# Issuing four read-back transfers behind the record of tile 47 in place of that of tile 49, in a fused scan and mixture-of-experts kernel

## The chip, the cores and the metric

The kernel runs on one core of one Trainium2 chip. The metric is the device time of one execution in microseconds (us), lower is better. Before the change three runs took 391.05, 392.11 and 394.93 us, a median of 392.11 us.

A core has five engines, each with an instruction queue of its own that runs in order: TensorE (PE, with weight loads shown as PEld), VectorE (DVE), ScalarE (ACT), GpSimd (POOL) and SyncE (SP). An engine at a wait does nothing of what stands behind that wait. SP issues nearly all the plain transfers (its row of the trace is called SPq), POOL the indirect ones.

## The reference, cut to what matters

The input is x of shape (8, 512, 128). It is normalised, and the result goes two ways: through a gated state-space branch with a recurrence over 512 time steps, and through a feed-forward branch with a top-2 mixture of 8 experts.

```python
def step(state, bc):                       # the recurrence, a state of 64 numbers per batch
    b_t, c_t = bc
    s = state @ A_bar + b_t
    s = _layernorm(s, ln_st_g, ln_st_b)
    return (s, c_t * s)

topw, topi = jax.lax.top_k(logits, K)      # K = 2 of E = 8
topw = jax.nn.softmax(topw, axis=-1)
w_dense = jnp.sum(jax.nn.one_hot(topi, E, dtype=xn.dtype) * topw[..., None], axis=-2)
h = _gelu(jnp.einsum('bsd,edh->ebsh', xn, ew1) + eb1[:, None, None, :])
eo = jnp.einsum('ebsh,ehd->ebsd', h, ew2) + eb2[:, None, None, :]
moe_out = jnp.einsum('ebsd,bse->bsd', eo, w_dense)
...
gate = jax.nn.sigmoid(combined @ gc_w + gc_b)
mixed = abel_out * (1.0 - gate) + moe_out * gate
...
x = x + s * g                              # s: state-space branch, g: silu of the expert branch
```

## The kernel before

**The recurrence.** The 512 steps of each batch are cut into 16 segments (`SEG`), so 128 segments of 32 steps run side by side, one in each partition, and the pass over the 32 steps is repeated in 5 rounds so that the segments' starts settle. That makes 148 steps in a row. One step is a small matrix product on PE (`tensor_step`, L1086), then on DVE the next state (L999) and its transpose `wT` (L987), which the next product waits for. Between two rounds there is a boundary (L1091, L1092 and the DVE work behind them).

**The experts.** Every token has two experts. Token rows are sorted by expert into tiles of 128 rows, in two halves of 39 tiles (`HALF_TILES`): tiles 0 to 38 are the first four batches, 39 to 77 the last four. A tile needs one *record*, the weights of its expert (`record<-experts`, a transfer by `fetch(g)`, five places in `record`), and its sorted rows (`desk<-sorted_rows` in the rows of the trace, `load_rows(c)` for three tiles at a time, 128 x 3 x 129 numbers of four bytes, which is 193.5 KB). On PE a tile is `rows_transpose` (L1520), `layer1` (L1527, the first instruction that reads the record) and `layer2` (L1537 and L1538, which raises `rows_done`). POOL then writes the finished rows back to their tokens' places in DRAM (`rows_back`, L1748, in the order of the tiles).

**What sets the order.** PE, ACT, DVE and POOL walk through the 148 steps in program order, and fixed tables say what stands behind the small product of a step t. `SLOT_AT` places the tiles: the slot with number j runs `layer1(j - 2)`, `rows_transpose(j)` and `layer2(j - 3)`. For the place in question:

| step t | what PE does behind the product of that step |
|---|---|
| 74, 75, 76, 77, 78 | slots 45 to 49: layer1 of tiles 43 to 47, layer2 of tiles 42 to 46 |
| 79 | no slot; `C_proj(0)` (L1512) |
| 80, 81, 82, 83 | slots 50 to 53: layer1 of tiles 48 to 51 |
| then | boundary of the round |

**The mix.** Once all tiles of a half are back in DRAM, `pull(n)` reads the two expert rows of every token of batch n (L1804, 516 KB each, destination `pulls[:, n % 4]`). `pull(0)` first waits until all rows of tiles 0 to 38 have landed (L1800). DVE's `factor_part(dve, n, 0)` (L1245) is the first reader, at step `MIX_AT[n]`: 79, 86, 93 and 100 for batches 0 to 3. It stands inside step 79, ahead of that step's L999.

**SP's queue.** SP's loop over the tiles g issues `fetch(g + 5)`, which waits for `rows_done` of tile g (that is, for layer2 of tile g), at every third g also `load_rows(g // 3 + 3)`, and at one g the four pulls of the first half:

```python
for g in range(TILES):
    if g + RECORDS < TILES:
        fetch(g + RECORDS)
    if g % CHUNK == 0 and g // CHUNK + 3 < TILES // CHUNK:
        load_rows(g // CHUNK + 3)
    if g == HALF_TILES + 5:
        for n in range(NB // HALVES):
            pull(n)
```

With `HALF_TILES` = 39 the pulls come at g = 44, behind the record of tile 49. The chunk of rows issued at g = 42 is number 17, that at g = 45 is number 18 (tiles 54 to 56).

Of the kernel before, what the change touches and what calls it, by code (L numbers as in the profile page):

```python
# [40 lines left out]
def build(nc, I, out):  # L41
    NB, T, H = I["L0_attn_x"].shape
    S = I["L0_attn_A"].shape[0]
    E, _, F = I["L0_ffn_ew1"].shape
    NROT = I["L0_ffn_gens"].shape[0]
    K = F // P
# [6 lines left out]
    HALF_TILES = Q * P * 2 // ROWS + E - 1  # L53
# [9 lines left out]
    with ExitStack() as ctx:  # L63
        sems = {}

        def sem(name):
            if name not in sems:
                sems[name] = ctx.enter_context(nc.semaphore(name))
            return sems[name]
# [1099 lines left out]
        def fallback(eng, one_round, redo):  # L1169

            eng.wait_ge(sem("agreed"), 1)
            settled = eng.value_load(agreed[0:1, 0:1], min_val=0, max_val=1)
            with eng.If(settled < 1):
                if one_round is not None:
                    with eng.Fori(0, SEG) as r:
                        one_round(eng, r)
                redo(eng)
            eng.end_ifs()
# [83 lines left out]
        def value_part(dve, n, i):  # L1262
            _, _, _, a, rest_g = factors(n)
            v = values[n % 4]
            part, s = divmod(i, SUB)
            if i == 0:
                dve.wait_ge(sem("factor"), factors_before(n) + 5)
                dve.wait_ge(sem("mix_rows"), n + 1)
            elif s == 0:
                dve.wait_ge(sem("value_part"), 2 * n + part)  # L1270
            if part < 2:
                t = dve.scalar_tensor_tensor(out=v[:, s, :], in0=pulls[:, n % 4, s, part, 0:P], scalar=a[:, s, part:part + 1], in1=v[:, s, :],
                                             op0=ALU.mult, op1=ALU.add)
                if s == SUB - 1:
                    t.then_inc(sem("value_part"), 1)
            else:
                t = dve.scalar_tensor_tensor(out=v[:, s, :], in0=abel[:, n, s, :], scalar=rest_g[:, s:s + 1], in1=v[:, s, :],
                                             op0=ALU.mult, op1=ALU.add)
                if s == SUB - 1:
                    t.then_inc(sem("ffn"), 1)  # L1280
# [5 lines left out]
        def summed_part(dve, n, s):  # L1286
            _, _, _, _, twice_g = factors(n)
            v = values[n % 4]
            if s == 0:
                dve.wait_ge(sem("factor"), factors_before(n) + 4)  # L1290
                dve.wait_ge(sem("base"), n - SUMMED + 1)
                dve.wait_ge(sem("summed"), n - SUMMED + 1)
            t = dve.scalar_tensor_tensor(out=v[:, s, :], in0=summed_bank(n)[:, s * P:(s + 1) * P], scalar=twice_g[:, s:s + 1], in1=v[:, s, :],
                                         op0=ALU.mult, op1=ALU.add)
            if s == SUB - 1:
                t.then_inc(sem("ffn"), 1)
# [143 lines left out]
        def store(sp, again, n):  # L1440
            sp.wait_ge(sem("final_rows"), NB * again + n + 1)
            sp.dma_start(out.rearrange("b (q k) h -> (b q) k h", k=L)[:, n * SUB:(n + 1) * SUB, :], outb[:, n]).then_inc(sem("out_stored"), 16)
# [41 lines left out]
        with nc.Block() as block:  # L1484
# [291 lines left out]
            @block.sync  # L1776
            def _(sp):
                def fetch(g):
                    e = sp.value_load(expert_of[0:1, g:g + 1], min_val=0, max_val=E - 1)
                    if g >= RECORDS:  # L1780
                        sp.wait_ge(sem("rows_done"), g - RECORDS + 1)
                    sp.dma_start(record[:, g % RECORDS], experts[:, ds(e, 1), :].squeeze(1)).then_inc(sem(f"record{g % RECORDS}"), 16)

                def load_rows(c):
                    h, t = divmod(c * CHUNK, HALF_TILES)
                    if t == 0:
                        sp.wait_ge(sem(f"scattered{h}"), 16 * 2 * Q)
                    if c >= 3:
                        sp.wait_ge(sem("rows_seen"), (c - 2) * CHUNK)
                        sp.wait_ge(sem("token_rows"), c - 2)  # L1790
                    at = (c % 3) * CHUNK
                    sp.dma_start(rows_in[:, at:at + CHUNK, :], sorted_rows[h][t * ROWS:(t + CHUNK) * ROWS, :].rearrange("(c p) h -> p c h", p=P))\
                      .then_inc(sem(f"rows_in{c % 3}"), 16)

                def pull(n):
                    h, i = divmod(n, NB // HALVES)
                    if i == 0:
                        for p in range(OUT_PLACES):
                            done = len(range(p, (h + 1) * HALF_TILES, OUT_PLACES))
                            sp.wait_ge(sem(f"rows_out{p}"), 16 * done)  # L1800
                    if n >= 4:
                        sp.wait_ge(sem("ffn"), n - 3)
                    first = JUNK + i * 2 * T
                    sp.dma_start(pulls[:, n % 4], token_rows[h][first:first + 2 * T, :].rearrange("(p s j) w -> p s j w", p=P, j=2)).then_inc(sem(f"pulled{n % 4}"), 16)  # L1804

                front_sync(sp)
                sp.wait_ge(sem("ew1_loaded"), 16)
                sp.wait_ge(sem("ew2r_ready"), E)
                sp.wait_ge(sem("eb2_stored"), 32)
                sp.wait_ge(sem("slots_ready"), 1)  # L1810
                sp.wait_ge(sem("tiles_known"), 2)
                for g in range(RECORDS):
                    fetch(g)
                for c in range(3):
                    load_rows(c)
                for g in range(TILES):
                    if g + RECORDS < TILES:
                        fetch(g + RECORDS)
                    if g % CHUNK == 0 and g // CHUNK + 3 < TILES // CHUNK:
                        load_rows(g // CHUNK + 3)  # L1820
                    if g == HALF_TILES + 5:
                        for n in range(NB // HALVES):
                            pull(n)
                for n in range(NB // HALVES, NB):
                    pull(n)
                for n in range(NB):
                    store(sp, 0, n)
                fallback(sp, None, store_redo)
                sp.wait_ge(sem("out_stored"), 16 * NB)
# [28 lines left out]
```

## Time and profile before

| | |
|---|---|
| three runs | 391.05, 392.11, 394.93 us |
| the profiled execution | 391.37 us, of which the span of the trace 389.5 us |
| mean granted TensorE clock | 0.907 of full speed |
| PE busy | 323.7 us (83%) |
| PEld busy | 250.0 us (64%) |
| DVE busy | 285.1 us (73%) |
| ACT busy | 190.8 us (49%) |
| POOL busy | 162.1 us (42%) |
| SP's DMA queue (q1) | 42.52 MB, 37.7% of the 16 DMA engines |
| POOL's DMA queue (q0) | 9.39 MB, 7.5% |

Times inside the trace count from the start of the span. A timeline row gives the start, the length, the engine, the line of the kernel and the operation, and in brackets how long the engine had been idle before it and what ended that idle time. In the row of an SP transfer the length is that of issuing; when the data has landed is another number ("to landing", counted from the issue's start). PEclk of 1.00 is the full clock of 2.4 GHz, 0.50 is 1.2 GHz.

### The profile page before, as it was taken

What the parts mean: (1) busy time and instruction counts of PE and PEld (TensorE: products, weight loads), DVE (VectorE), ACT (ScalarE), POOL (GpSimd) and SP (SyncE); (2) the same over time, 40 slices, a digit from 0 to 9 for tenths busy, and PEclk for the clock granted to TensorE, in tenths of its full rate; (3) what the DMA queues carried; (4) which work ended last, traced back from release to release, by engine and by line L of the source; (5) the groups of instructions that cost most, each with busy time, mean ns of one, the idle gap of its engine ahead of it and who ended that gap; (6) DMA issues with size and microseconds to landing.
All of it is one profiled execution on the core that took longest, in us unless ns stands there. A gap on an engine that the chain in (4) does not pass through costs nothing.

```text
span 389.5 us, 11592 instructions
## 1 busy us (share of the span) xinstructions
PE 323.7 (83%) x4002; PEld 250.0 (64%) x4014; DVE 285.1 (73%) x1320; ACT 190.8 (49%) x563; POOL 162.1 (42%) x225
## 2 busy tenths in 40 slices
PE   1886988967988869999989999889999988878770
PEld 0676975667555547887777887667767746656450
DVE  2787546999388776888857665669899755788972
ACT  1142982500033325666637668458776628565310
POOL 8051000016777777777776554335554500000000
PEclk9998995865599988999989999889999988999996
DMA  8449990001511314767757667946665224000102
GB/s 276 96 138 199 171 143 0 2 3 34 200 56 57 112 56 162 248 228 248 240 179 234 229 223 241 329 141 210 226 204 211 70 68 164 29 29 29 40 18 87
DMA packets 44158, 54.80 MB, mean 141 GB/s; under 512 B 6841, under 2 KB 28768, under 8 KB 44096
## 3 DMA queue, kind: packets, MB, share of 16 engines
q1 hardware_dynamic: 38975, 42.52, 37.7%
q0 software_dynamic: 4544, 9.39, 7.5%
q10 hardware_dynamic: 576, 2.10, 1.5%
q8 instruction: 35, 0.57, 0.6%
q14 instruction: 28, 0.22, 0.2%
HBM read 14.15 MB, written 16.63 MB: 79 GB/s over the span
## 4 chain that ended last, share of the span: by engine, by line
PE 59%; DVE 24%; issue 5%; ACT 5%; DMA 3%; SPq 2%; DVEq 0%; ACTq 0%
PE bank L1086 11%; PE bank L1527 11%; PE bank L1537 8%; PE bank L1557 2%; PE bank L1490 2%; DVE wT L987 2%; PE bank L1520 2%; PE bank L1505 2%; PE bank L1497 2%; DMA record<-experts 2%; PE bank L459 2%; PE bank L419 2%; PE bank L1426 2%; PE bank L1512 2%; PE bank L445 1%
## 5 line engine op out<-in xcount | busy, mean ns | idle before, releaser
L1748 POOL DMA_INDIRECT token_rows<-rows_out,token_rows_i x78 | 75.7, 971 | 64.2 <-ACT rows_out L1659 27.4
L1086 PE MATMUL bank<-Mrep,wT 32*32 32x64 f32 x2368 | 65.4, 225 | 17.9 <-DVE wT L987 17.6
L1086 PEld LDWEIGHTS bank<-Mrep,wT 32*32 32x32 f32 x2368 | 41.7, 107 | 55.5 <-issue 53.3
L1734 POOL DMA_INDIRECT sorted_rows<-late,slots x64 | 62.7, 980 | 28.4 <-issue 14.5
L1652 ACT ACTIVATE desk<-bank,record 128x128 f32<-128x128 f32 x156 | 48.8, 364 | 44.5 <-PE bank L1527 44.1
L1527 PE MATMUL bank<-desk,record 128*128 128x128 f32 x312 | 58.6, 313 | 0.1
L999 DVE SCALAR_TENSOR_TENSOR ring<-bank,Rho,Dv 128x64 f32<-128x64 f32 x112 | 31.8, 284 | 26.8 <-PE bank L1086 24.4
L1537 PE MATMUL bank<-record,desk 128*128 128x129 f32 x312 | 50.3, 285 | 0.0
L1527 PEld LDWEIGHTS bank<-desk,record 128*128 128x128 f32 x312 | 43.1, 200 | 7.9 <-issue 1.2
L1537 PEld LDWEIGHTS bank<-record,desk 128*128 128x128 f32 x312 | 43.4, 201 | 0.2
L1644 ACT ACTIVATE desk<-bank,cols 128x128 f32<-128x128 f32 x78 | 35.9, 460 | 3.0 <-PE bank L1520 3.0
L987 DVE STREAM_TRANSPOSE wT<-ring 128x64 f32<-128x64 f32 x112 | 27.5, 245 | 3.5
L1520 PE MATMUL bank<-ident,desk 128*128 128x128 f32 x78 | 22.4, 287 | 1.4 <-ACT desk L1644 1.4
L1659 ACT COPY rows_out<-bank 128x129 f32<-128x129 f32 x78 | 21.3, 273 | 4.3 <-PE bank L1538 4.3
L973 DVE CUSTOM_DVE_ANT_0 sqj<-ring,guess 128x64 f32<-128x64 f32 x64 | 19.6, 306 | 0.1
L459 PE MATMUL bank<-desk 128*128 128x128 f32 x72 | 13.2, 339 | 7.0 <-DVE desk L770 4.9
L1538 PE MATMUL bank<-record,ones 128*128 128x129 bf16 x78 | 17.7, 227 | 0.0
L999 DVE SCALAR_TENSOR_TENSOR late<-bank,Rho,Dv 128x64 f32<-128x64 f32 x31 | 8.7, 281 | 11.3 <-PE bank L1086 11.3
L459 PEld LDWEIGHTS bank<-desk 128*128 128x128 f32 x72 | 11.4, 241 | 8.6 <-DVE desk L770 6.4
L1557 PE MATMUL bank<-bias,ones 128*128 128x512 bf16 x46 | 15.1, 449 | 2.1 <-issue 2.1
L419 PE MATMUL bank<-B_wT,gi 128*128 128x64 f32 x64 | 12.8, 385 | 3.6 <-DVE Dv L712 3.6
L419 PEld LDWEIGHTS bank<-B_wT,gi 128*128 128x128 f32 x64 | 12.5, 297 | 4.2 <-DVE gi L707 3.7
(333 smaller groups left out, 635.9 us busy)
## 6 DMA issues: line engine op xcount, KB each, us to landing
record<-experts SPq DMA_DIRECT2D x78, 290.5 KB
sorted_rows<-zero_rows SPq DMA_DIRECT2D x2, 2515.5 KB, 28.3
desk<-sorted_rows SPq DMA_DIRECT2D x26, 193.5 KB
pulls<-token_rows SPq DMA_DIRECT2D x8, 516.0 KB, 5.4
X<-in_L_attn_x ACTq DMA_DIRECT2D x4, 512.0 KB, 6.2
out<-xT SPq DMA_DIRECT2D x8, 256.0 KB, 2.0
token_rows<-rows_out,token_rows_i POOLq DMA_INDIRECT x78
experts<-in_L_ffn_ew SPq DMA_DIRECT2D x1, 1024.0 KB, 6.4
```

The source lines that it names most:

```text
L419: t = pe.matmul(banks[bank][:, k * S:(k + 1) * S], x, w, start=True, stop=True)
L459: t = pe.matmul(banks[1][:, m * P:(m + 1) * P], XT[:, m, :], EX[:, m, :], start=True, stop=True)
L987: dve.transpose(wT[:, :], prev).then_inc(sem("state_T"), 1)
L999: dve.scalar_tensor_tensor(out=state(r, k), in0=psY, scalar=Rho[:, k:k + 1], in1=Dv[:, k, :], op0=ALU.mult, op1=ALU.add).then_inc(sem("sta ...
L1086: t = pe.matmul(psY[q], wT[q, 32 * c:32 * c + 32], Mrep[q, c, :], start=(c == 0), stop=(c == 1))
L1520: pe.transpose(bank_in[:, 0:P], rows_in[:, g % (3 * CHUNK), 0:P], ident[:, :]).then_inc(sem("rows_seen"), 1)
L1527: t = pe.matmul(hidden_bank(g)[:, k * P:(k + 1) * P], w[:, k * P:(k + 1) * P], rows_T[:, g % 2, :], start=True, stop=True)
L1537: pe.matmul(o, hidden[:, g % 2, k, :], w[k], start=(k == 0), stop=False)
L1644: act.activation(rows_T[:, g % 2, :], bank_in[:, 0:P], ACT.Identity, scale=col["ln_gamma"], bias=col["ln_beta"]).then_inc(sem("rows_T"), 1)
L1652: t = act.activation(hidden[:, g % 2, k, :], hidden_bank(g)[:, k * P:(k + 1) * P], ACT.Gelu, bias=bias[:, k:k + 1])
L1734: pool.indirect_dma_start(sorted_rows[h], bass.IndirectOffsetOnAxis(ap=slots[:, j, q:q + 1], axis=0), sort_rows[:, q, :], None)\
L1748: pool.indirect_dma_start(token_rows[h], bass.IndirectOffsetOnAxis(ap=token_rows_i[:, g:g + 1], axis=0), rows_out[:, g % OUT_PLACES, :], N ...
```

## The change

The four pulls move from iteration g = 44 to g = 42 of SP's loop.

```diff
@@ -1818,7 +1818,7 @@
                         fetch(g + RECORDS)
                     if g % CHUNK == 0 and g // CHUNK + 3 < TILES // CHUNK:
                         load_rows(g // CHUNK + 3)
-                    if g == HALF_TILES + 5:
+                    if g == HALF_TILES + 3:
                         for n in range(NB // HALVES):
                             pull(n)
                 for n in range(NB // HALVES, NB):
```

The instructions of PE, DVE, ACT and POOL stay the same and in the same order. On SP, around iterations 42 to 45, two records change places with the pulls. The row that opens this piece of the difference is the load of rows chunk 17; the rows with a minus are the records of tiles 48 and 49 (a register load of the expert's number, and the transfer), where they stood before:

```order
 L1792 DMA desk<-sorted_rows 128x3x129
-L1779 TENSOR_LOAD expert_of
-L1779 ISA x2
-L1782 ISA
-L1782 DMA record<-experts 128x581
-L1779 TENSOR_LOAD expert_of
-L1779 ISA x2
-L1782 ISA
-L1782 DMA record<-experts 128x581
 L1804 DMA pulls<-token_rows 128x1032 x4
```

In the changed kernel nothing stands between chunk 17 and the pulls, and the same two records, marked with a plus, come behind them, ahead of the record of tile 50, which opens with the last two rows:

```order
 L1804 DMA pulls<-token_rows 128x1032 x4
+L1779 TENSOR_LOAD expert_of
+L1779 ISA x2
+L1782 ISA
+L1782 DMA record<-experts 128x581
+L1779 TENSOR_LOAD expert_of
+L1779 ISA x2
+L1782 ISA
+L1782 DMA record<-experts 128x581
 L1779 TENSOR_LOAD expert_of
 L1779 ISA x2
```

So each pull is issued two records earlier in SP's order, and the records of tiles 48 and 49 four pulls later.

## Rows read from the trace of the kernel before

**Rows 1.** The page, chain that ended last: share of the span by engine.
```profile
PE 59%; DVE 24%; issue 5%; ACT 5%; DMA 3%; SPq 2%; DVEq 0%; ACTq 0%
```

**Rows 2.** Timeline of DVE at step 79.
```profile
241.29 0.16 DVE L951 SCALAR_TENSOR_TENSOR Rho<-roots,Rho 128x1 f32<-128x1 f32 x1
243.93 0.17 DVE L1245 TENSOR_TENSOR gains<-pulls,weights 128x8 f32<-128x8 f32 x1 [2.48 <-DMA pulls<-token_rows]
```

**Rows 3.** Timeline of PE, layer1 of tiles 47, 48, 49, 50 and between.
```profile
240.01 0.71 PE L1527 MATMUL bank<-desk,record 128*128 128x128 f32 x4
...
241.62 1.12 PE L1512 MATMUL bank<-xaT,C_wT 128*128 128x512 f32 x2
244.73 0.43 PE L1086 MATMUL bank<-Mrep,wT 32*32 32x64 f32 x16 [1.98 <-DVE wT L987]
245.08 1.13 PE L1527 MATMUL bank<-desk,record 128*128 128x128 f32 x4
...
247.91 1.04 PE L1527 MATMUL bank<-desk,record 128*128 128x128 f32 x4
...
250.00 0.71 PE L1527 MATMUL bank<-desk,record 128*128 128x128 f32 x4
```

**Rows 4.** Timeline of SP: record 47, rows chunk 17, records 48, 49, first pull.
```profile
235.01 0.49 SPq L1782 DMA_DIRECT2D record<-experts  x1
235.60 0.53 SPq L1792 DMA_DIRECT2D desk<-sorted_rows  x1
237.16 0.50 SPq L1782 DMA_DIRECT2D record<-experts  x1
238.36 0.50 SPq L1782 DMA_DIRECT2D record<-experts  x1
239.05 0.45 SPq L1804 DMA_DIRECT2D pulls<-token_rows  x1
```

**Rows 5.** Chain in order of time: issue of pull 3, then record 50.
```profile
241.74 0.43 SPq L1804
...
242.88 7.08 DMA record<-experts
```

**Rows 6.** Issue to landing of pull 0, then of pull 3, each asked alone.
```profile
DMA to landing us min/median/max: 4.9/4.9/4.9
...
DMA to landing us min/median/max: 7.4/7.4/7.4
```

**Rows 7.** The page, DMA issues: number and size of each.
```profile
record<-experts SPq DMA_DIRECT2D x78, 290.5 KB
...
pulls<-token_rows SPq DMA_DIRECT2D x8, 516.0 KB, 5.4
```

**Rows 8.** Windows: length; busy time of five engines; PEclk, DMA share, GB/s.
```profile
236.00:238.00 2.00, 2.00 (x31) 1.63 (x30) 1.47 (x9) 1.52 (x6) 1.14 (x2) 1.00 0.87 267
238.00:240.00 2.00, 2.00 (x44) 1.62 (x42) 1.28 (x8) 1.52 (x6) 1.35 (x2) 1.00 0.76 273
241.00:249.00 8.00, 6.02 (x70) 4.40 (x69) 3.60 (x24) 3.98 (x14) 2.46 (x3) 0.79 0.98 319
246.00:248.00 2.00, 2.00 (x24) 1.52 (x23) 0.49 (x5) 1.24 (x4) 0.00 (x0) 0.50 0.97 267
```

**Rows 9.** Timeline of POOL: the write-back of tile 38, and that of tile 77.
```profile
228.34 0.96 POOL L1748 DMA_INDIRECT token_rows<-rows_out,token_rows_i  x1 [0.65 <-issue]
...
315.94 0.96 POOL L1748 DMA_INDIRECT token_rows<-rows_out,token_rows_i  x1 [4.82 <-PE bank L1086]
```

**Rows 10.** The second half's pulls: first issue, its landing, all pulls, last two landings.
```profile
318.51 0.34 SPq L1804 DMA_DIRECT2D pulls<-token_rows  x1
DMA to landing us min/median/max: 3.5/3.5/3.5
...
L1804 SPq DMA_DIRECT2D pulls<-token_rows x8: 340/432/1366, 239.0 to 319.8; - x8
...
DMA to landing us min/median/max: 5.2/5.6/6.0
```

## The prediction

> **What bounds the kernel now.** I read the chain that ended last first. PE and DVE hold 83% of it [rows 1]: the recurrence with the expert tiles packed between its steps. The DMA has 3%, but the chain has a piece that is a transfer: the record issued at 242.88 us, 7.08 us long [rows 5]. So the place to look at is 235 to 250 us.
>
> There I read the timelines of DVE and PE. DVE ends L951 of step 79 at 241.45 us and stands still for 2.48 us until pull 0 has landed [rows 2]. PE, which ends `C_proj(0)` at about 242.74 us (241.62 + 1.12), gets its next state late and idles 1.98 us; step 80 starts at 244.73 and layer1 of tile 48 at 245.08 [rows 3]. The stall has a second price. The granted clock reads 0.50 at 246 to 248 us [rows 8]: PE had been without work and then ran at 1.2 GHz. Layer1 takes 1.13 and 1.04 us in place of 0.71, and from layer1 of tile 48 to that of 49 it is 2.83 us, from 49 to 50 2.09 us, where a slot at full clock takes 1.61 (240.01 to 241.62) [rows 3]. The last 0.1 to 0.2 us of the 2.09 is the record of tile 50, which landed at 242.88 + 7.08 = 249.96 us, and PE's layer1 of tile 50 starts at 250.00 [rows 3, 5].
>
> Next SP and its queue. SP issues record 47 at 235.01, rows chunk 17 at 235.60, records 48 and 49 at 237.16 and 238.36, and pull 0 at 239.05 [rows 4]. Pull 0 lands 4.9 us later, at 243.95 (DVE starts at 243.93), pull 3 at 241.74 + 7.4 = 249.14 [rows 5, 6], and record 50, issued behind it, 0.82 us after pull 3. The landings are in the order of issue: a record of 290.5 KB does not pass the pulls of 516 KB ahead of it [rows 7]. Pulls land (249.14 - 243.95) / 3 = 1.73 us apart. The DMA engines are 98% busy at 241 to 249 us [rows 8]. They are a full pipe here, and the change alters who is served first in it.
>
> **What the change does, step by step.** No instruction is added or removed, so no engine's work costs anything new. Four pulls move ahead of two records (each a register load, three small register instructions and one DMA), past no other queue than SP's.
>
> *Pull 0 earlier.* Behind chunk 17, whose issue ends at 236.13, and with the 0.19 us that lie between the end of record 49's issue (238.86) and pull 0 now, pull 0 is issued at 236.32, 2.73 us earlier [rows 4]. Is its wait (all rows of the first half back in DRAM) met by then? Tile 77's write-back starts at 315.94 and the pulls that wait for it follow at 318.51, so 2.57 us from start to landing [rows 9, 10]. Tile 38's starts at 228.34, so its rows are back at about 230.9, and with twice that latency at 233.5. No wait there. In front of pull 0 in the queue are only record 47 and chunk 17. They are 484 KB, and the engines moved 267 GB/s x 2 us = 534 KB at 236 to 238 us [rows 8], so the queue is free for pull 0 from about 237.9. At 1.73 us a pull, and about 1.0 us from the last byte to the semaphore (my estimate: record 47 is issued at 235.01 and the 236 to 238 window holds its bytes, so a transfer starts about 1 us after its issue; I take as much at its end), pull 0 lands at about 240.7. From below it can't be quicker than the 3.5 us of the undisturbed pull [rows 10], 239.8; with the old 4.9 us it is 241.2. DVE asks at 241.45: all are earlier. **The 2.48 us wait of DVE goes.**
>
> *What is late next.* Without it step 80 stands ready when `C_proj(0)` ends (L999 follows its product by about 0.6 us and the transpose is done at about 242.4), so PE starts step 80 at about 242.7 and asks for the record of tile 48 at about 243.0. That is 2.0 us earlier than now. Going on at full clock, layer1 of tile 50 would come at 243.0 + 2 x 1.61 = 246.3 in place of 250.0: the whole worth of the stall is 3.7 us, 2.0 directly and 1.7 for the low clock and the late record 50.
>
> *The records' price.* The four pulls hold SP from 239.05 to 242.88 now, 3.83 us, so record 48 is issued at 236.32 + 3.83 = 240.15 in place of 237.16. That alone would do no harm. But it is served behind all four pulls. I size its landing in two ways. From the front: 237.9 + 4 x 1.73 + 0.82 for the record + 1.0 = 246.6. From the back: pull 3 lands at 249.14 now with records 48 and 49 ahead of it; take out 2 x 0.82, and the 0.24 x 2 = 0.5 us in which the engines are idle at 238 to 240 [rows 8], because the next transfer is not issued yet: 247.0, and record 48 at 247.8. I take **247.2**. Record 49 follows at 248.0, and record 50 at about 249 to 249.5, slightly earlier than now, since the same bytes go through a pipe that starts a little earlier. PE stands at layer1 of tile 48 from 243.0 to 247.2, **4.2 us** in place of the 1.98 us now. Behind that instruction on PE stand rows_transpose, layer2 of tile 47 and the product of step 81, and DVE waits for that product. Layer1 of tile 48 comes at 247.2 in place of 245.1: **+2.1 us**.
>
> *After it.* Record 49 is there before PE asks for it (247.2 + at least 1.61 = 248.8). Record 50 is too, which gives back **0.15**. The clock falls for this gap as it did for the old one. If it stays low equally long counted from the return of work, the cost is the same; if counted from the gap, up to 2 us of it now pass in the stall. I take back **0.3** of at most 0.7 (2 us at the relation 1.61 to 2.83, less what overlaps with other work). The later pulls (1 to 3) are wanted from step 86 on and have their cover. The chain behind is PE and DVE, so the shift is carried to the end.
>
> *Sum.* +2.1 - 0.15 - 0.3 = +1.65 us on the profiled execution's own 391.37 us (span 389.5 and 1.9 around it): **393.0 us**. That execution is 0.7 under the median of the three runs, 392.11, and their spread of 391.05 to 394.93 is wider than the effect.
>
> **A rule beside the rows.** The rows show that record 50 landed behind pull 3, in issue order. The Trainium skill, "DMA: Bandwidth & Descriptors", section on queues, rings and completion order, says that each DMA engine consumes the descriptors of one queue in ring order; the trace agrees (0.82 us behind pull 3). The same page, section "Anatomy of one DMA", fits a transfer as about 2.0 us plus its bytes over 436 GB/s (for the GpSimd path). An estimate by that page: a pull every 1.2 us, record 48 there at about 236.3 + 2.0 + 4 x 1.21 + 0.68 = 243.8, a stall of 0.8 us only and 2.9 us gained, 388.4 us. The trace disagrees at this place: 319 GB/s at 98% busy [rows 8].
>
> **Rivals.**
>
> *Faster a little: the pulls flow as in the second half.* There the first lands at 322.0 and the last at 319.8 + 6.0 = 325.8, 1.27 us apart [rows 10]. Then record 48 lands at 237.9 + 4 x 1.27 + 0.75 + 1.0 = 244.7, 0.4 us before layer1 of tile 48 runs now; with record 50 in time -0.5 us: 390.8. Against it: nothing else moved at 318 us, while at 237 to 245 POOL's write-backs go on. If still quicker, the gain grows to the next rival's. The Trainium skill's fit, named above, is this mechanism taken further: its 388.4 lies between this rival and the next, inside their 0.27.
>
> *Faster: the records are not held.* If record 48 shared the engines with the pulls and landed by 243.0, the change would bring the whole 3.7 us: 387.7. Record 50, behind pull 3 now, speaks against it. It decides whether the change gains: the break-even is a landing of record 48 at about 245.2.
>
> *The change does nothing.* Pull 0 and record 48 trade one stall for an equal one, with record 48 at about 245.2 to 245.7: 391.4 to 391.9. It is the low edge of my forecast's own range (391.5 to 394.5).
>
> *Slower by more: the clock doesn't recover.* The longer gap ends about 6 us ahead of the round's boundary, which has a gap of its own. If the clock stays at 1.2 GHz between them, three more slots take about 2.8 in place of 1.6 us, +3.6: 396.7. Against it: the clock was back by 250.00 (0.71 us) after the old gap [rows 3].
>
> **How the numbers follow.** Chances: the forecast 0.60 (the equal trade in it), faster a little 0.17, records not held 0.10, clock not back 0.13. The range takes the forecast, the first rival and the bounds on the drain: 389.8 to 395.5. Faster by over 1%, about what a measurement of this kernel can tell from no change, is under 388.2 and needs nearly the whole 3.7 us: 0.04. Slower by over 1% is over 396.0 and needs the clock: 0.08. The rest, 0.88, is within 1%.
>
> **What the changed profile would show.** Right: SP issues pull 0 at about 236.3; no wait of DVE's L1245 on the pulls; PE's idle time of about 4 us now before layer1 of tile 48, put down to the record and not to `wT`; record 48's landing at about 247. The forecast falls if L1527 has no such wait or one under 2 us (then the pipe drains faster, or not in order), and it is too small if records 49 or 51 are waited for as well, or if the clock is low for over 4 us behind the gap.

## The result, and the profile after

The changed kernel is slower by less than 1%: the ratio of its times to those before is 1.0089, with a 95% interval of 1.0062 to 1.0116, from 22 runs of each. That ratio, like the others below, leaves out the runs that lie far above the fastest of their kernel, which are many of those of before and few of the changed kernel's, so it need not agree with the medians. Over all 22 runs the medians are 395.62 us (393.21 to 399.92) and 394.83 us (388.82 to 396.94), 0.8 us apart, and the means 395.95 and 393.89 us, 2.1 us apart. The three runs shown at first, with their median of 392.11, lay at the low side of what the kernel before does. The profiled execution took 395.0 us, its span 393.1.

| | before | after |
|---|---|---|
| profiled execution / span | 391.37 / 389.5 us | 395.0 / 393.1 us |
| mean granted clock | 0.907 | 0.898 |
| PE busy | 323.7 us | 326.2 us |
| DVE busy | 285.1 us | 285.2 us |

SP's timeline after the change (start, length of issuing, line, operation) has the pulls behind chunk 17 of the rows, and the three records after them:

```profile
235.26 0.49 SPq L1782 DMA_DIRECT2D record<-experts  x1
235.85 0.53 SPq L1792 DMA_DIRECT2D desk<-sorted_rows  x1
236.57 1.84 SPq L1804 DMA_DIRECT2D pulls<-token_rows  x4
239.11 3.24 SPq L1782 DMA_DIRECT2D record<-experts  x3
```

DVE's first reader of pull 0 no longer has a wait (its row of before is in [rows 2]):

```profile
241.61 0.16 DVE L1245 TENSOR_TENSOR gains<-pulls,weights 128x8 f32<-128x8 f32 x1
```

PE's timeline from step 79 to the boundary of the round, to be read against [rows 3]. L1512 is `C_proj(0)`, the L1527 rows are layer1 of tiles 48, 49 and 50, and L1091 opens the boundary:

```profile
241.87 1.13 PE L1512 MATMUL bank<-xaT,C_wT 128*128 128x512 f32 x2
242.93 0.43 PE L1086 MATMUL bank<-Mrep,wT 32*32 32x64 f32 x16
247.72 1.22 PE L1527 MATMUL bank<-desk,record 128*128 128x128 f32 x4 [4.37 <-DMA record<-experts]
...
250.63 1.22 PE L1527 MATMUL bank<-desk,record 128*128 128x128 f32 x4
...
252.81 0.71 PE L1527 MATMUL bank<-desk,record 128*128 128x128 f32 x4
...
256.05 0.43 PE L1091 MATMUL bank<-ends,shift 128*128 128x64 f32 x2 [0.30 <-DVE ends L1009]
```

Step 80 starts 1.8 us earlier than before (242.93 for 244.73), and then PE stands for 4.37 us in front of layer1 of tile 48, until the record of that tile has landed (in the kernel before that instruction waited for nothing, [rows 3]). The chain in order of time has the same transfer, 8.56 us from issue to landing, in place of the record of tile 50 in [rows 5]:

```profile
239.11 8.56 DMA record<-experts
```

So it landed at 247.67. Pull 2 and pull 3, issued at 237.47 and 237.94, took (each asked alone)

```profile
DMA to landing us min/median/max: 7.9/7.9/7.9
...
DMA to landing us min/median/max: 8.8/8.8/8.8
```

and landed at 245.4 and 246.7. The record is 0.9 us behind the last pull, in the order of issue.

The packets of the queue say the same. A pull is 128 packets of 4128 bytes and a record 128 of 2324 bytes, so each can be told in the trace. The first packets of the four pulls start at 238.02, 239.75, 241.67 and 243.68 us, and that of record 48 at 245.06, although it was issued at 239.11. Pull 0's last packet ends at 240.49. Its landing has no row of its own, but DVE's reader had no wait at 241.61.

**A measure of the place alone.** The boundary of the kernel before opens with

```profile
253.24 0.43 PE L1091 MATMUL bank<-ends,shift 128*128 128x64 f32 x2 [0.30 <-DVE ends L1009]
```

From the start of `C_proj(0)` to the start of the boundary (L1512 to L1091), which I call the place from here on, the kernel before needs 253.24 - 241.62 = 11.62 us, the changed one 256.05 - 241.87 = 14.18 us: **+2.56 us**. This stretch holds both waits and the low clock right behind them, and it varies little, as the experiments show. What the clock does behind the boundary isn't in it. The rest of the +3.6 us of span is elsewhere: 0.25 us before step 79, and the remainder behind the boundary, where the two executions differ in where the clock is low. At the end, the last batch's products on PE are

```profile
382.45 2.08 PE L1426 MATMUL bank<-D_wT,late 128*128 128x128 f32 x8
```

after the change, where the first profile of before has 1.16 us for the same eight.

### The profile page after: what moved, and what is told of

It is laid out like the page before. It is cut to its first block, busy times and chain, and to the rows that moved or that the text cites. A ratio compares the mean times of both kernels' runs of the same rounds, so it can differ in the third digit from the quotient of the medians.

```text
span 393.1 us, 11592 instructions
## 1 busy us (share of the span) xinstructions
PE 326.2 (83%) x4002; PEld 251.9 (64%) x4014; DVE 285.2 (73%) x1320; ACT 191.0 (49%) x563; POOL 161.6 (41%) x225
## 4 chain that ended last, share of the span: by engine, by line
PE 60%; DVE 23%; issue 5%; ACT 5%; DMA 4%; SPq 1%; DVEq 0%; ACTq 0%
PE bank L1086 11%; PE bank L1527 11%; PE bank L1537 8%; PE bank L1426 2%; PE bank L1490 2%; PE bank L1497 2%; DMA record<-experts 2%; DVE wT L987 2%; PE bank L1557 2%; PE bank L1520 2%; PE bank L1505 2%; PE bank L419 2%; PE bank L459 2%; PE bank L1512 2%; PE bank L445 1%
## 5 line engine op out<-in xcount | busy, mean ns | idle before, releaser
L1527 PE MATMUL bank<-desk,record 128*128 128x128 f32 x312 | 58.8, 314 | 4.6 <-DMA record<-experts 4.4
L1527 PEld LDWEIGHTS bank<-desk,record 128*128 128x128 f32 x312 | 43.3, 201 | 12.3 <-DMA record<-experts 4.5
L419 PEld LDWEIGHTS bank<-B_wT,gi 128*128 128x128 f32 x64 | 12.2, 291 | 4.7 <-DVE gi L707 4.2
```

The source lines that it names most:

```text
L419: t = pe.matmul(banks[bank][:, k * S:(k + 1) * S], x, w, start=True, stop=True)
L1527: t = pe.matmul(hidden_bank(g)[:, k * P:(k + 1) * P], w[:, k * P:(k + 1) * P], rows_T[:, g % 2, :], start=True, stop=True)
```

## The experiments

All kernels but three differ from the kernel before only in the iteration g of SP's loop at which each pull is issued; the three have added products on PE as well. In the diffs the key is g - 39. The kernels were timed in three series, each with runs of the kernel before beside them, so the medians of before differ from one to another.

**The changed kernel again** (no edit).

> The changed kernel once more, unaltered. My account so far: layer1 of tile 48 waits for its record (4.4 us, landing at about 247.7), 2.6 us are lost by the end of that round, and what the first profile lost beyond it (to +3.6 us of span) came from where the granted clock was low later: not low around 327 to 330 us (0.8 us won), low from 378 us on (1.5 us lost). Theory A (the late clock lows fall where they fall, by chance or by how the program lies in time): the wait of 4 to 5 us and the loss of 2.4 to 2.8 us by the boundary repeat, the late lows may differ. Theory B (the lows belong to the change): the last eight products (L1426) again take about 2.08 us. Time against before: +2 to +4 us.

```profile
243.09 1.12 PE L1512 MATMUL bank<-xaT,C_wT 128*128 128x512 f32 x2
...
250.00 1.22 PE L1527 MATMUL bank<-desk,record 128*128 128x128 f32 x4 [5.44 <-DMA record<-experts]
...
258.01 0.43 PE L1091 MATMUL bank<-ends,shift 128*128 128x64 f32 x2 [0.30 <-DVE ends L1009]
```

The middle row is PE's layer1 of tile 48 in the second profile, of an execution of 396.7 us. The wait is longer still, 5.44 us. Each asked alone, pulls 0 and 3, issued at 237.80 and 239.2, took

```profile
DMA to landing us min/median/max: 4.7/4.7/4.7
...
DMA to landing us min/median/max: 10.0/10.0/10.0
```

The queue did not send more slowly: record 48's first packet starts at 246.19, 8.4 us after the issue of pull 0, where it was 8.5 us in the first profile. The record then took 3.8 us from its first packet to its landing at 249.96, in place of 2.6. What held its last packets I haven't found.

The place costs 14.92 us here, +3.3, over the upper end of the 2.4 to 2.8 I had named. The last products take 1.16 us and not 2.08, and in the fourth profile of the kernel before, shown further down, they take 2.08, so theory B falls: the low clock at the end does not belong to the change. The time was 395.91 us (12 runs) against 395.58 for before (35), ratio 1.0037 (0.9995 to 1.0079). The +2 to +4 us that I had named for the whole time did not show in the medians.

**Pull 0 early, the rest at the boundary.**

```diff
-                    if g == HALF_TILES + 5:
-                        for n in range(NB // HALVES):
-                            pull(n)
+                    for n in {3: (0,), 11: (1, 2), 12: (3,)}.get(g - HALF_TILES, ()):
+                        pull(n)
```

> Pull 0 behind the record of tile 47 as in the change, pulls 1 and 2 at g = 50 and pull 3 at g = 51, in the lull at the round's boundary. In-order queue with 1.7 us a pull: record 48 stands behind one pull and lands by about 241.5 to 242, before PE asks for it at 243.0 to 243.3, and record 50 has no pull ahead but pull 0, so neither stall is left: layer1 of tile 50 at about 246.5, 3.5 us earlier than in before, total 3 to 4 us under before. Rival (records are late for another reason than the pulls ahead of them, such as SP's own issue time): PE still waits 2 us or more at layer1 of tile 48, gain under 1.5 us. Second rival: the pulls at the boundary hold record 52 or later, and 1 to 3 us come back there.

```profile
242.01 0.16 DVE L1245 TENSOR_TENSOR gains<-pulls,weights 128x8 f32<-128x8 f32 x1
...
242.22 1.12 PE L1512 MATMUL bank<-xaT,C_wT 128*128 128x512 f32 x2
243.63 0.71 PE L1527 MATMUL bank<-desk,record 128*128 128x128 f32 x4
...
246.85 0.71 PE L1527 MATMUL bank<-desk,record 128*128 128x128 f32 x4
...
250.08 0.43 PE L1091 MATMUL bank<-ends,shift 128*128 128x64 f32 x2 [0.29 <-DVE ends L1009]
```

DVE's reader of pull 0 has no wait, and PE's timeline shows layer1 of tiles 48 and 50 with no wait in front and at full clock. The place takes 7.86 us, **3.76 less than before**, which is the 3.7 us at which the prediction had put the whole stall. The time is 390.22 us (12 runs) against 395.58, ratio 0.9935 (0.9889 to 0.9982): faster than both kernels, by 5.4 us in the medians and about 2.5 by the ratio, around the 3 to 4 us expected. Only the order of the transfers has changed, so it was the three later pulls ahead of the records that did the harm, and PE waits for no record further on.

**Pull 0 early, the rest where they were.** The table is `{3: (0,), 5: (1, 2, 3)}`.

> Pull 0 behind the record of tile 47, pulls 1 to 3 stay behind that of tile 49. In-order queue: DVE's wait goes, record 48 is in time, but record 50 has still all four pulls ahead of it and lands at about 249.0 to 249.5, while PE now asks for it at about 246.3: a wait of 2.5 to 3.2 us at layer1 of tile 50 and a time about equal to before (-1.0 to +0.5 us). Rival (a record is not held by pulls ahead of it, only record 48's late issue did the harm): no such wait, 3 to 4 us under before.

```profile
249.94 1.22 PE L1527 MATMUL bank<-desk,record 128*128 128x128 f32 x4 [3.03 <-DMA record<-experts]
```

This row of PE is layer1 of tile 50; those of 48 and 49 wait for nothing. The wait has gone to the record behind the pulls, 3.03 us where 2.5 to 3.2 were expected. The clock falls behind it, the place takes 12.84 us, and the time is unchanged: ratio 1.0015 (0.9963 to 1.0067). In front of DVE's L1245 a wait of 0.28 us was left.

**Pull 0 where it was, the rest at the boundary.** The table is `{5: (0,), 11: (1, 2), 12: (3,)}`.

> Pull 0 stays behind the record of tile 49 as in before, pulls 1 to 3 go to the boundary (g = 50, 51). In-order queue: DVE's wait on pull 0 stays at 2.5 us and the clock falls after it as in before, record 50 has one pull ahead of it and is not waited for (0.15 us). Time within 0.5 us of before. It separates pull 0's lateness from the crowd behind it: if the wait on pull 0 shrinks to under 1.5 us, later transfers slow the ones ahead of them, and the queue is not served in order.

```profile
243.74 0.17 DVE L1245 TENSOR_TENSOR gains<-pulls,weights 128x8 f32<-128x8 f32 x1 [2.77 <-DMA pulls<-token_rows]
```

DVE waits 2.77 us for pull 0 with no other pull behind it (2.48 before): later transfers do not slow the earlier one. The time is 1.0035 (0.998 to 1.0091) of before. One thing came out otherwise. The record of tile 50 isn't waited for any more, and still the place takes 13.05 us, 1.4 more than before. Layer1 of tile 48 comes 0.5 us later from the start of `C_proj(0)` (245.12 - 241.14, against 3.46), and 0.9 us is the clock, which stayed low for two whole slots in place of one and a part: layer1 of tiles 48, 49 and 50 starts at 245.12, 248.03 and 250.95.

**Three pulls early, and two.** The tables are `{3: (0, 1, 2), 11: (3,)}` here and `{3: (0, 1), 11: (2,), 12: (3,)}` further down.

> Pulls 0 to 2 behind the record of tile 47, pull 3 at g = 51 at the boundary. In-order queue at 1.7 to 1.9 us a pull: record 48 lands one pull earlier than in the changed kernel, and PE waits 4.4 to 5.4 less 1.8, so 2.5 to 3.5 us at layer1 of tile 48. Time within 1 us of before. Rival (the queue sends them together, or record 48 waits for something that follows the first pull only): the wait stays over 4 us or is gone.

```profile
245.51 0.71 PE L1527 MATMUL bank<-desk,record 128*128 128x128 f32 x4 [2.90 <-DMA record<-experts]
```

> Pulls 0 and 1 behind the record of tile 47, pull 2 at g = 50, pull 3 at g = 51. In-order queue: one pull less ahead of record 48 than with three (wait 2.9 us), so a wait of 0.6 to 1.4 us at layer1 of tile 48, too short for the clock to fall in front of the boundary. Time 1.5 to 3.5 us under before, 0.5 to 1.5 us over the kernel that sends only pull 0 early. Rival (the records' lateness comes in a step, not by the number of pulls): no wait at all, or again over 2 us.

```profile
244.70 0.71 PE L1527 MATMUL bank<-desk,record 128*128 128x128 f32 x4 [1.10 <-DMA record<-experts]
```

Both rows are PE's layer1 of tile 48. The waits, 2.90 and 1.10 us, fall into the expected 2.5 to 3.5 and 0.6 to 1.4. With the rows of the other kernels this gives the price of a pull ahead of a record. The last column is read from the packets: from the first packet of pull 0 to the first packet of record 48.

| pulls ahead of record 48 | pull 0 issued | record 48 landed | between | wait of PE | first packet to first packet |
|---|---|---|---|---|---|
| 1 (pull 0 early, rest at the boundary) | 236.92 | not waited for | | none | 1.58 us |
| 2 | 236.17 | 244.66 | 8.5 us | 1.10 us | 3.48 us |
| 3 | 235.51 | 245.46 | 9.9 us | 2.90 us | 5.48 us |
| 4 (the change) | 236.57 | 247.67 | 11.1 us | 4.37 us | 7.04 us |
| 4 (the change again) | 237.80 | 249.96 | 12.2 us | 5.44 us | 6.99 us |

By the landings a pull costs 1.2 to 1.5 us on the faster rows and 2.2 with the repeat, but a landing also holds the time that the last packets need, and that differs from profile to profile. By the first packets a pull takes 1.6 to 1.8 us of the queue in each of them. The low clock came later behind the wait of 2.90 us than behind the one of 4.37: layer1 of tile 48 is at full clock, and those of tiles 49 and 50 take 1.15 and 1.02 us. Three early: 395.38 us (10 runs) against 394.47, ratio 1.0075 (1.003 to 1.0121). Two early: 390.73 us (4 runs) against 396.25, ratio 0.9815 (0.9741 to 0.9889), which would be more than the expected 3.5 us. With four runs, one of them at 398.35, the size is not settled; the 2.3 us that the place gains is the firmer figure.

**Work for PE in the gap: the changed kernel.** `keep_warm(n, bank)` gives PE n products whose result nobody reads. The difference is against the changed kernel.

```diff
                         C_proj(C_AT[t])
+                        if C_AT[t] == 0:
+                            keep_warm(16, 6)
```

> The changed kernel with 16 more products that nobody reads behind C_proj(0), so that PE has work for about 3.5 us of its wait. If the clock falls because PE stands without work there, layer1 of tiles 48 to 50 runs at 0.71 us, layer1 of tile 50 comes 3.3 us behind that of tile 48 in place of 5.1, and the wait on record 48 is about 1 to 2 us after the added products, with its landing where it was: 1.5 to 2.5 us under the changed kernel. Rival (the low clock has its own time and does not follow from the gap): 2.8 to 2.9 us from layer1 to layer1 as before, no gain.

```profile
249.06 0.71 PE L1527 MATMUL bank<-desk,record 128*128 128x128 f32 x4 [1.07 <-DMA record<-experts]
...
252.28 0.71 PE L1527 MATMUL bank<-desk,record 128*128 128x128 f32 x4
...
255.52 0.43 PE L1091 MATMUL bank<-ends,shift 128*128 128x64 f32 x2 [0.30 <-DVE ends L1009]
```

The record is as late as ever (8.70 us from issue to landing, at 249.0), but PE has stood idle for 1.07 us only, and layer1 of tiles 48 to 50 runs at full clock, 3.22 us from first to third. The place takes 12.46 us, 1.7 to 2.5 less than the changed kernel. The time is 393.22 us (10 runs), 2.4 to 2.7 under the changed kernel's medians, which are of other series; against its own series of before it is 1.3 us under in the medians, ratio 1.0031 (0.9972 to 1.009). So in this place the gap causes the low clock that follows it, as the next kernel shows a second time.

**The same for the kernel before**, with `keep_warm(8, 6)`.

> The kernel before with 8 such products behind C_proj(0): PE has work for 1.75 of its 1.98 us. If the gap causes the low clock, layer1 of tile 48 starts at the same place and the next two slots take 1.6 us each, 1.5 us under before or more; record 50 (landing at about 249.9) is then waited for about 1.5 us, which eats the gain: 0 to 1.5 us under before. Rival (the clock does not follow from the gap): the slots stay at 2.8 and 2.1 us.

```profile
244.87 0.71 PE L1527 MATMUL bank<-desk,record 128*128 128x128 f32 x4
...
250.15 0.72 PE L1527 MATMUL bank<-desk,record 128*128 128x128 f32 x4 [1.99 <-DMA record<-experts]
...
252.57 1.22 PE L1527 MATMUL bank<-desk,record 128*128 128x128 f32 x4
```

The first part holds: no low clock behind the added products. But PE now reaches layer1 of tile 50 early, waits 1.99 us for its record, and the clock falls behind that wait instead. The place takes 13.32 us, 1.7 more than before, where I had expected a small gain; the time is 1.0036 (0.9979 to 1.0094) of before. To speed PE up ahead of a transfer that is late only moves the wait.

**The kernel before again**, three more profiles.

> The kernel before once more, unaltered, for a second profile of it. Its first profiled execution took 391.37 us, the median of its later runs is 394.8 to 395.6. Theory A (the length and the number of stretches at the low clock differ from execution to execution, and the first profile had short ones): the wait of DVE on pull 0 is 2 to 3 us again, but the stretch at 1.2 GHz behind it, or another one later, is longer, and an execution of about 395 us shows at least 2 us more of products at the low clock. Theory B (the runs of 395 us have a longer wait on pull 0, since the transfers are slower there): the wait is 4 us or more.

> A third profile of the kernel before, to see what an execution of 395 us or more has in it. If the low stretches decide: either the stretch behind the wait on pull 0 lasts about twice as long as in the first profile (over 6 us in place of under 4), or there is one more later, and it takes 3 us or more longer than the first profiled execution at 391.37. If the transfers decide: the wait on pull 0 or on record 50 is over 4 us, with the same low stretches.

> A fourth profile of the kernel before, with the same two accounts as for the third. An execution of 390 to 392 us should have low stretches like those of the first profile, one of 394 or more a longer or a further one; in both the wait on pull 0 is 2.4 to 3.0 us.

The executions took 392.8, 396.88 and 393.27 us. The wait of DVE on pull 0 is 2.79, 2.52 and 2.32 us (the last a little under the 2.4 named), and the place takes 11.74, 11.64 and 11.48 us: the same in an execution of 397 as in one of 391. In the execution of 396.88 us the row is

```profile
244.55 0.17 DVE L1245 TENSOR_TENSOR gains<-pulls,weights 128x8 f32<-128x8 f32 x1 [2.52 <-DMA pulls<-token_rows]
```

What differs is the clock later on. In the windows of two stretches (length, busy time of PE, PEld, DVE, ACT and POOL, PEclk, DMA share, GB/s), first the profile of 391.37 us:

```profile
320.00:340.00 20.00, 16.25 (x223) 11.85 (x213) 13.62 (x67) 12.40 (x40) 0.00 (x0) 0.91 0.29 115
360.00:386.00 26.00, 14.28 (x191) 9.32 (x193) 18.95 (x74) 4.34 (x12) 0.00 (x0) 0.92 0.14 54
```

and that of 396.88 us:

```profile
320.00:340.00 20.00, 16.25 (x211) 11.55 (x214) 12.25 (x63) 10.76 (x33) 0.00 (x0) 0.83 0.29 107
360.00:386.00 26.00, 21.41 (x220) 14.11 (x220) 19.86 (x81) 5.52 (x15) 0.00 (x0) 0.74 0.07 25
```

From L1091 at the boundary to the end of the span it is 136.3 us in the one and 141.2 us in the other, 4.9 of the 5.5 us between them. Theory A stands for this pair; the profiles of 392.8 and 393.27 us by themselves decided nothing. What makes the clock fall in the one execution and not in the other I haven't found.

The second profile came with nine more runs. Their median with it is 396.53 us, where 31 other runs of the same kernel in the same series have 394.47: with nothing changed, the median of ten runs lies 2.1 us off (the ratio is 1.0006, 0.9913 to 1.01).

**Pull 0 early, the rest at the boundary, and work for PE at two boundaries.**

```diff
                     if k == L - 1:
                         tensor_boundary(pe, turn + 1)
+                        if ROUNDS - 3 <= r < ROUNDS - 1:
+                            keep_warm(6, 6)
```

> The kernel with pull 0 early and the others at the boundary, and 6 products that nobody reads in PE's gap at the boundaries behind steps 83 and 115. If the low clock follows from PE's gaps, the two stretches at 1.2 GHz that the kernel without them shows (about 252 to 256 and 310 to 314 us) are gone or moved, worth 1 to 1.5 us each where PE bounds: 386 to 389 us, 1 to 3 us under the kernel without them. Rival (a low stretch only moves to the next gap of PE): same low time in sum, no gain within 1 us.

The columns are those of the windows above.

```profile
252.00:260.00 8.00, 7.91 (x103) 5.37 (x102) 7.05 (x41) 5.16 (x17) 2.77 (x4) 1.00 0.92 296
...
310.00:320.00 10.00, 8.97 (x119) 4.26 (x123) 6.70 (x37) 3.65 (x11) 1.92 (x2) 1.00 0.18 47
...
340.00:350.00 10.00, 7.76 (x81) 5.65 (x81) 7.40 (x32) 6.34 (x20) 0.00 (x0) 0.77 0.08 29
```

In these windows the clock is full at both boundaries, where the kernel without the added products reads 0.79 and 0.83. But it reads 0.77 at 340 to 350 us, where the other has 1.00, and 0.91 at 260 to 280. The time is 390.67 us (6 runs) against 396.25, 5.6 us under before in its series, where the kernel without the added products was 5.4 under in its own: no gain within 1 us, as the rival had it. That the low stretches moved on because of the added products isn't shown. The profile is of the slowest of the six runs (393.51 us), low stretches come and go between executions of one kernel, and the window 252 to 260 us is at full clock too in the changed kernel with work in the gap and in the kernel with three pulls early, which have no work at the boundary.

The place, from L1512 to L1091, in all profiles:

| kernel | us | against before |
|---|---|---|
| before (four profiles) | 11.62, 11.74, 11.64, 11.48 | |
| changed (two) | 14.18, 14.92 | +2.6, +3.3 |
| changed, with work in the gap | 12.46 | +0.8 |
| three pulls early | 12.38 | +0.8 |
| two pulls early | 9.37 | -2.3 |
| pull 0 early, rest at the boundary | 7.86 | -3.8 |
| the same, with work at the boundaries | 8.35 | -3.3 |
| pull 0 early, rest unchanged | 12.84 | +1.2 |
| rest at the boundary, pull 0 unchanged | 13.05 | +1.4 |
| before, with work in the gap | 13.32 | +1.7 |

## Why the prediction was wrong in size, point by point

**Right: pull 0.** It was issued at 236.57 (forecast 236.32) with no wait for the rows of the first half, and the wait of 2.48 us on DVE went. The forecast of 240.7 means 4.4 us from issue to landing, and there is little to spare: it took 4.7 us in the repeat and in the kernel with three pulls early, and between 5.4 and 6.2 in three of the kernels with one or two early. DVE still waited 0.62 us in the kernel with two.

**Right: where the stall goes.** PE waits for the record of tile 48, behind all four pulls in the queue, for more than it had lost before. The kernels with one, two, three and four pulls ahead of it, and the one in which the wait moved to record 50, show the order of service; the rival in which the records are not held falls. So does the rival in which the pulls flow as in the second half. From the first packet of pull 0 to that of record 48 each pull took 1.76 us in the changed kernel and 1.75 in its repeat, near my 1.73 and not its 1.27, nor the 1.21 of the estimate that gave 388.4. My landing of 247.2 lay 10.9 us behind the issue of pull 0; measured are 11.1 and 12.2 us.

**Wrong: the term of the landing.** "Layer1 of tile 48 comes at 247.2 in place of 245.1: +2.1 us." From the start of `C_proj(0)` to layer1 of tile 48 it is 5.85 us in the changed kernel and 6.91 in its repeat, 3.46 before (3.31 to 3.78 in the four profiles): **+2.39 and +3.45 us**. The wait measured 4.37 and 5.44 us against 4.2. The pace of the queue was right. What I had as one fixed number is the time from a record's first packet to its landing: 0.82 + 1.0 us in the sum from the front, 2.4 us with the 247.2 that I took, and 2.6 and 3.8 us in the two profiles.

**Wrong: what comes back after it.** "Record 50 is too, which gives back 0.15", and "I take back 0.3" for the clock: -0.45 us. From layer1 of tile 48 to that of tile 50 the changed kernel took 5.09 us and 4.77 in its repeat, 4.92 before: **+0.17 and -0.15**. Both lie in or near what the four profiles of before span by themselves (4.73 to 4.93), so the term is about nothing. Record 50 was in time, but the clock stayed low past the return of work as long as before (2.91 us and then 2.18 for two slots, 2.83 and 2.09 before). With the landing this makes +2.6 and +3.3 us in place of +1.65.

**Wrong: the base.** This is the step that put the measured time outside the range. I summed on the profiled execution's 391.37 us, which is 3.5 us under the 394.83 of the same series, and gave a range by the mechanisms alone. The text said that the spread of the three runs was wider than the effect, and then did nothing with it. The kernel before has its median at 394.5 to 396.3 us in the later series; a forecast of the same +1.65 would have stood at 396.5 us on the 394.83, and at 396 to 398 on those. The 395.62 us measured lie just above my range's 395.5. The miss of 2.6 us (395.62 against 393.0) is 3.5 us of base, less the 0.9 us by which the difference of the medians, 0.8 us, stays under my +1.65. That it is so near the range's end is luck: the two partly cancel. The difference of the two full medians, 0.8 us (2.1 of the means), is smaller than +2.6 to +3.3 at the place. Since the spread from the clock behind the boundary is up to 5 us, I don't read the difference as a gain given back there; it isn't settled.

**The slower rival** (the clock stays low up to the boundary) did not come: the slot of tile 50 ran at full clock, 252.81 to 254.42.

## What to carry to other kernels

When a large transfer is moved ahead in a queue, write down for each transfer that it passes when its data is wanted, and charge it with everything now in front. Here a wait of 2.5 us was exchanged for one of 4.4 to 5.4, while sending only the transfer that was wanted early, and the other three where nothing was in a hurry, removed the wait altogether and took 3.8 us from the place. Judge such a change by the stretch it touches (here 11.5 to 11.7 us in four profiles), since the whole kernel's time spreads over more than the effect. And put a forecast on the median of many runs, not on the one execution that was profiled.

## What the runs showed of the hardware

The clock of TensorE after a gap carries a price beyond the gap. Behind the wait of 4.37 us two slots took 2.91 and 2.18 us where 1.61 is the full-clock time, and with added products in the gap (1.07 us idle) 1.61 each. Behind a wait of 2.90 us the first slot still took 1.61 us, and the next two 2.84 and 1.92. At which later gaps it falls differs between executions of one and the same kernel: 136.3 against 141.2 us for the same work behind the boundary.

The queue of SP served its transfers in the order of issue, and beside the other traffic a 516 KB pull took 1.6 to 1.8 us of it, from first packet to first packet, in the kernel before and in the five rows of the table. When nothing else moved the four landed 1.27 us apart [rows 10]. Landings spread more than that: from pull 0 to pull 3 they lay 1.73 us apart in the first profile of before [rows 6] and 2.2 us in the repeat of the changed kernel (pull 0 at 242.5, pull 3 at 249.2, so 6.7 / 3), and record 48 landed 2.6 us after its first packet in one profile and 3.8 in another. One profile gives the pace well, and a landing to about 1 us.
